# A three-block transformer kernel: expert stage and second attention merged into one block, with the first tile's steps, the gathers and the last key/value stores reordered

## The reference, cut to what matters

```
x = x + attention0(layernorm(x), ctx, ctx)   # 8 heads over the 512 axis, softmax over 64
x = x + experts(layernorm(x))                # gate x @ W_gate, top 2 of 8, mean of relu(x @ W_e + b_e)
x = x + attention1(layernorm(x), ctx, ctx)   # 32 query heads in 8 groups, head size 16, 64 keys
x = x + ffn(layernorm(x))                    # silu(x Wg + bg) * (x Wu + bu), inner size 1376, then Wd
```

## Time and profile before

| | us |
|---|---|
| median of 3 runs (lowest to highest) | 917.22 (916.62 to 917.77) |
| the profiled execution, its own time | 916.35 |
| its span, first to last instruction | 914.6 |
| PE busy | 861.1 (94%) |
| DVE, ACT, POOL busy | 442.5, 347.7, 296.6 |
| mean granted TensorE clock | 0.984 |
| first attention, first to last matmul (about) | 0 to 164 |
| experts, first matmul to last add | 173.5 to 303.2 |
| second attention, first matmul to the last scores | 307.0 to 525.7 |

### The profile page before, as it was taken

How to read it: one execution, slowest core, us unless ns; L and a number is a source line. 1 busy time by engine, 2 the same in 40 slices (tenths; PEclk the granted TensorE clock), 3 DMA queues, 4 the chain that set the end, 5 groups by cost and what they waited for, 6 DMA issues and landing times.

```text
span 914.6 us, 19686 instructions
## 1 busy us (share of the span) xinstructions
PE 861.1 (94%) x7537; PEld 698.9 (76%) x7537; DVE 442.5 (48%) x898; ACT 347.7 (38%) x567; POOL 296.6 (32%) x413
## 2 busy tenths in 40 slices
PE   6999998599999769999999899999999999999997
PEld 4788887478888757777777688887888788878885
DVE  3988886244444557887888741212221222222112
ACT  3555654233333245666666542221222122211111
POOL 3587885000000477777765231112020002002000
PEclk9999999799999898999999999999999999999999
DMA  8556666687553433554432341110030003002001
GB/s 284 175 185 235 214 206 228 217 271 247 165 173 127 150 93 126 150 154 130 137 91 56 100 160 40 47 43 1 13 104 24 0 12 104 1 1 92 1 1 46
DMA packets 55084, 105.24 MB, mean 115 GB/s; under 512 B 8050, under 2 KB 12146, under 8 KB 54866
## 3 DMA queue, kind: packets, MB, share of 16 engines
q1 hardware_dynamic: 48226, 84.98, 28.9%
q0 software_dynamic: 5120, 16.78, 5.5%
q10 hardware_dynamic: 1648, 2.23, 0.7%
HBM read 67.99 MB, written 35.98 MB: 114 GB/s over the span
## 4 chain that ended last, share of the span: by engine, by line
PE 61%; ACT 2%; DVE 1%; issue 1%; POOL 1%; DMA 1%; DVEq 0%; POOLq 0%
PE c_ps L1238 9%; PE c_ps L1240 9%; PE c_ps L1239 9%; PE c_bank L1719 4%; PE c_bank L1277 3%; PE c_bank L1276 3%; PE c_bank L1282 3%; PE c_bank L1720 3%; PE c_bank L1724 3%; PE c_bank L1779 3%; PE c_po L1795 2%; PE c_ps L1754 2%; PE c_po L1282 1%; PE c_po L1277 1%; PE c_po L1276 1%; ACT c_probT L1628 1%
## 5 line engine op out<-in xcount | busy, mean ns | idle before, releaser
L1315 DVE SCALAR_TENSOR_TENSOR d_hid<-c_ps,d_b_up,d_silu 128x512 f32<-128x512 f32 (+1 forms) x44 | 33.0, 750 | 229.7 <-PE c_ps L1240 229.7
L1238 PE MATMUL c_ps<-d_nT_hi,gate_up_hi 128*128 128x512 f32 (+1 forms) x352 | 140.1, 398 | 0.0
L1240 PE MATMUL c_ps<-d_nT_hi,gate_up_lo 128*128 128x512 f32 (+1 forms) x352 | 138.5, 394 | 0.0
L1239 PE MATMUL c_ps<-d_nT_lo,gate_up_hi 128*128 128x512 f32 (+1 forms) x352 | 138.3, 393 | 0.0
L1194 ACT ACTIVATE d_silu<-c_ps,d_b_gate 128x512 f32<-128x512 f32 (+1 forms) x44 | 30.3, 688 | 141.7 <-PE c_ps L1240 141.7
L1509 POOL DMA_INDIRECT c_y_in<-expert_results,y_at x32 | 36.6, 1145 | 145.2 <-POOLq L99 137.2
L1154 POOL TENSOR_TENSOR late_x<-late_x,d_b_down 128x512 f32<-128x512 f32 x16 | 21.6, 1380 | 188.0 <-DMA late_x<-x_after_attention 188.0
L1240 PEld LDWEIGHTS c_ps<-d_nT_hi,gate_up_lo 128*128 128x128 f32 (+1 forms) x352 | 65.2, 185 | 16.6
L1239 PEld LDWEIGHTS c_ps<-d_nT_lo,gate_up_hi 128*128 128x128 f32 (+1 forms) x352 | 65.4, 186 | 15.9
L1238 PEld LDWEIGHTS c_ps<-d_nT_hi,gate_up_hi 128*128 128x128 f32 (+1 forms) x352 | 65.2, 185 | 15.4
L1201 ACT ACTIVATE d_hid_hi<-d_hid 128x512 fp32r<-128x512 f32 (+1 forms) x44 | 27.8, 632 | 125.6 <-DVE d_hid L1315 125.6
(11 more groups left out here) (272 smaller groups left out, 1937.5 us busy)
## 6 DMA issues: line engine op xcount, KB each, us to landing
b_rows<-expert_rows SPq DMA_DIRECT2D x39, 256.0 KB, 2.8
expert_results<-b_result SPq DMA_DIRECT2D x39, 256.0 KB, 2.5
a_wstage<-L_ffn_W_e SPq DMA_DIRECT2D x16, 512.0 KB, 4.0
late_x<-x_after_attention SPq DMA_DIRECT2D x28, 256.0 KB, 3.9
c_stage<-gate_up SPq DMA_DIRECT2D x16, 344.0 KB, 3.2
out<-late_x SPq DMA_DIRECT2D x16, 256.0 KB, 2.9
x_after_attention<-late_x SPq DMA_DIRECT2D x12, 256.0 KB, 3.7
c_y_in<-x_after_attention SPq DMA_DIRECT2D x12, 256.0 KB, 2.8
```

Source lines behind the costliest of these rows:

```text
L1238: pe.matmul(bank[0:w, :], gu_hi[:, cols], nT_hi[:, g % 2, k, :], start=k == 0, stop=False)
L1239: pe.matmul(bank[0:w, :], gu_hi[:, cols], nT_lo[:, g % 2, k, :], start=False, stop=False)
L1240: mm = pe.matmul(bank[0:w, :], gu_lo[:, cols], nT_hi[:, g % 2, k, :], start=False, stop=k == KD - 1)
```

## The change

It does six things.

1. The experts no longer have a block of their own. `experts` returns functions for each engine, and the second attention's block runs them first. Their buffers lie on the same memory as the second attention's, their four PSUM banks are banks of the second attention, and their end is no barrier: PE waits for the DVE adds before it uses the last two banks, GpSimd and SP wait for the last stores (`ex.stored`), and GpSimd zeroes `kv` (before: DVE, L1930) once the last expert product is made. The clearing of the experts' semaphores between the stages is gone; a new set (`kept_`) adds one clearing at the program's end.
2. The first tile: its x comes by an earlier load; `add_first_rows` on DVE does the two adds of tile 0; GpSimd does `spread_keys(0)` and `scale_x2(0)` before `add_rows(1)` and `gather(2)`.
3. SP: the two halves of Wq are loaded during the experts into `late_x`; x tiles 2 to 5 and both halves of Wo follow behind the landing of `gather(0)`.
4. The splits of Wo move: ACT does both before the loop, DVE one before it and one in its first step. PE makes keys and values 0 to 6 before `transpose_x(0)` (before: 0 to 5), and those of tile 7 on the two sides of `make_q(0)`.
5. In each step PE does `transpose_probs(m, 0, 0)` before `scores(m, 1)`, and `gather(m + 5)` waits for `attend(m, 0, 1)`.
6. First attention: the stores of keys and values are no longer awaited in their block; `score` joins as a third staging buffer, cleared on DVE at m = TILES; `keep_kv(2)`, the first to use it, waits for that clearing.

The diff, cut to its core (the experts' own loops are the same but for indentation and for the names of semaphores and banks):

```diff
-        kv_stage = (qT, kT)
+        kv_stage = (qT, kT, score)
...
             def store_kv(i):
                 sp.wait_ge(kv_kept, i + 1)
-                sp.dma_start(shared["kv"][i, :, :], kv_stage[i % 2][:, 0:KV_COLS]).then_inc(kv_stored[i % 2], 16)
+                sp.dma_start(shared["kv"][i, :, :], kv_stage[i % 3][:, 0:KV_COLS]).then_inc(kv_stored[i % 3], 16)
...
             sp.wait_ge(front_zeroed, 16)
             for i in range(2):
                 sp.wait_ge(x1_stored[i], 8 * TILES)
-                sp.wait_ge(kv_stored[i], 8 * KV_LATE)
...
-                if i < 2:
-                    act.wait_ge(kv_cleared, 6)
-                want(act, kv_stored[i % 2], 16 * (i // 2))
-                act.activation(kv_stage[i % 2][:, 0:P], bank[:, 0:P], ACT.Copy).then_inc(kv_step, 1)
-                values = kv_stage[i % 2][:, P:KV_COLS].rearrange("p (b j r d) -> p b j r d", b=2, j=4, r=2)
+                if i < 3:
+                    act.wait_ge(kv_cleared, 3 * max(i, 1) + 3)
+                want(act, kv_stored[i % 3], 16 * (i // 3))
+                act.activation(kv_stage[i % 3][:, 0:P], bank[:, 0:P], ACT.Copy).then_inc(kv_step, 1)
...
                     dve.wait_ge(s_made, TILES)
+                elif i == 2:
+                    dve.wait_ge(pt_made, TILES)
                 dve.memset(blocks, 0.0).then_inc(kv_cleared, 1)
...
+                if m == TILES:
+                    clear_kv_stage(2)
...
+    sem, sb = c.sem, Placed(nc, "b_", shared["base"] + 2 * 4 * 2 * EXPERTS * DIM).sb
...
+    pt, py = banks[0:2], banks[2:4]
...
+            if 2 <= n < 4:
+                sp.dma_start(late.x[:, n - 2, :], shared["x1"][n - 2, :, :]).then_inc(late.x_loaded[n - 2], 16)
+            if 4 <= n < 6:
+                half = n - 4
+                sp.dma_start(late.x[:, 2 * half + 2:2 * half + 4, :], wq_v[:, 2 * half:2 * half + 2, :]).then_inc(proj_loaded[half], 16)
...
+            act.wait_ge(biased_made, b + 1)
+            want(act, stored[b % 3], 16 * (b // 3))
+            if b == 0:
+                for i in range(3):
+                    act.wait_ge(shared["kv_stored"][i], 16 * ((KV_LATE + 2 - i) // 3))
+            act.activation(result[:, b % 3, :], biased[:, b % 2, :], ACT.Relu, scale=0.5).then_inc(result_made, 1)
...
 
-            return score[:, n, :] if n < 2 else stage[:, :, :].rearrange("p s n -> p (s n)")[:, 0:1024]
+            if n == 2:
+                return stage[:, :, :].rearrange("p s n -> p (s n)")[:, 0:1024]
+            return (late.x[:, 2:4, :], late.x[:, 4:6, :], None, x_more[:, :, :])[n].rearrange("p s n -> p (s n)")
...
             def load_weights(n):
-                if n == 3:
-                    sp.wait_ge(proj_lo_made, 3)
-                src = (wq_v, wo_v)[n // 2][:, 2 * (n % 2):2 * (n % 2) + 2, :]
+                src = wo_v[:, 2 * (n % 2):2 * (n % 2) + 2, :]
...
             def load_x1(t):
+                if t in (X_RING, X_RING + 1):
+                    sp.wait_ge(proj_lo_made, 4)
...
 
-            for n in range(4):
-                load_weights(n)
+            def load_late_x(t):
+                sp.wait_ge(proj_lo_made, t // 2)
+                sp.dma_start(late.x[:, t, :], shared["x1"][t, :, :]).then_inc(late.x_loaded[t], 16)
+
+            ex.sync(sp)
+            sp.wait_ge(y_loaded[0], 32)
+            load_late_x(2)
+            load_late_x(3)
+            load_weights(2)
+            for i in range(3):
+                sp.wait_ge(ex.stored[i], 16 * ((BLOCKS + 2 - i) // 3))
+            load_weights(3)
+            load_late_x(4)
+            load_late_x(5)
             load_gate_up(0)
             load_gate_up(1)
             for t in range(X_RING, RING):
...
+            def clear_values():
+                pool.wait_ge(ex.y_made, BLOCKS)
+                pool.memset(kv[:, :, P:KV_COLS], 0.0).then_inc(values_zeroed, 1)
+                pool.wait_ge(values_zeroed, 1)
+                for r in range(2):
+                    pool.memset(kv[64 * r:64 * r + 64, :, P:KV_COLS].rearrange("p s (n r d) -> p s n r d", r=2, d=HD + 1)[:, :, :, r, HD:HD + 1], 1.0).then_inc(values_zeroed, 1)
+                pool.wait_ge(values_zeroed, 3)
...
             def add_rows(t):
+                if t == 1:
+                    pool.wait_ge(x2_ready, 1)
...
+            make_constants()
+            clear_values()
+            for i in range(3):
+                pool.wait_ge(ex.stored[i], 16 * ((BLOCKS + 2 - i) // 3))
             gather(0)
             gather(1)
-            make_constants()
-            add_rows(0)
-            gather(2)
+            spread_keys(0)
             scale_x2(0)
             add_rows(1)
+            gather(2)
+            scale_x2(1)
             gather(3)
-            scale_x2(1)
-            spread_keys(0)
             for m in range(TILES + 2):
                 if m == 0:
                     add_rows(2)
@@ -1576,6 +1601,7 @@
...
                 if m + 5 < TILES:
+                    pool.wait_ge(o_made, 4 * m + 2)
                     gather(m + 5)
...
+            ex.scalar(act)
             keep_kT(0)
+            high_weights(0)
             keep_kT(1)
-            high_weights(0)
-            keep_kT(2)
             high_weights(1)
-            for t in (3, 4, 5):
+            for t in range(2, 7):
                 keep_kT(t)
             norm_x(0)
             keep_high_x(0)
-            keep_kT(6)
+            high_weights(2)
             keep_q_rows(0)
             norm_x(1)
             keep_kT(7)
             keep_q(0)
+            high_weights(3)
             for m in range(TILES + 2):
                 if m + 1 < TILES:
...
                 if m < TILES:
                     exponent(m, 0)
-                if m == 0:
-                    high_weights(2)
                 if m + 1 < TILES:
                     keep_q_rows(m + 1)
                 if m < TILES:
@@ -1672,9 +1697,7 @@
                     exponent(m, 1)
                     if m == TILES - 1:
...
+                if t == 4:
+                    pe.wait_ge(ex.biased_made, BLOCKS - 1)
...
-                make_kv(t)
-            pe.wait_ge(const_made, N_CONST)
+            ex.tensor(pe)
+            for t in range(7):
+                make_keys(t)
+                make_values(t)
             transpose_x(0)
-            make_kv(6)
+            make_keys(7)
             make_q(0)
-            make_kv(7)
+            make_values(7)
             transpose_q(0)
             for m in range(TILES + 1):
                 if m < TILES:
...
                 if m < TILES:
+                    transpose_probs(m, 0, 0)
                     scores(m, 1)
-                    transpose_probs(m, 0, 0)
                     transpose_probs(m, 0, 1)
...
+            def add_first_rows():
+                dve.wait_ge(late.x_loaded[0], 16)
+                dve.wait_ge(y_loaded[0], 32)
+                dve.tensor_tensor(x[0], x[0], y_in[:, 0, :], ALU.add).then_inc(x2_added, 1)
+                dve.wait_ge(x2_added, 1)
+                dve.tensor_tensor(x[0], x[0], y_in[:, 1, :], ALU.add).then_inc(x2_ready, 1)
+
+            ex.vector(dve)
             keep_values(0)
+            low_weights(0)
             keep_values(1)
-            low_weights(0)
+            low_weights(1)
             keep_values(2)
-            low_weights(1)
             keep_values(3)
-            keep_values(4)
+            add_first_rows()
             sum_x2(0)
             average_x2(0)
+            keep_values(4)
             keep_values(5)
+            keep_values(6)
             keep_low_x(0)
+            low_weights(2)
             sum_x2(1)
             average_x2(1)
-            keep_values(6)
             keep_values(7)
             for m in range(TILES + 2):
                 if 0 <= m - 2 < TILES:
@@ -1955,7 +1990,7 @@
                 if m + 1 < TILES:
...
                 if m == 0:
-                    low_weights(2)
+                    low_weights(3)
                     sum_x2(2)
                     average_x2(2)
...
+    shared["base"] = SBUF_END - nc.sbuf_bytes_remaining
     with ExitStack() as stack:
+        kept = Ctx(nc, stack, "kept_")
+        shared["kv_stored"] = [kept.sem(f"kv_stored{i}") for i in range(3)]
+        stack.callback(kept.clear)
         with ExitStack() as moe:
             shared["ex23"] = [moe.enter_context(nc.sbuf_tensor(f"expert_{n}", [P, 2 * EXPERTS * DIM], F32R)) for n in ("hi23", "lo23")]
             first_attention(nc, shared, shared["layer0"], shared["layer1"])
-            late = LateBuffers(nc, stack, shared, shared["layer1"])
-            experts(nc, shared, shared["b_e"], late)
+        late = LateBuffers(nc, stack, shared, shared["layer1"])
         second_attention(nc, shared, shared["layer1"], late, a, out)
 
 

```

265 lines of the change are left out of this document (123 added, 142 removed).

## The result

In the first comparison the changed kernel takes 911.28 us (median of 4, 910.36 to 911.67) and the kernel before 917.5: a ratio of 0.992, 95% interval 0.9893 to 0.9946. The forecast was 905.2 with 901.5 to 908.8; the result lies outside. The profiled execution of the changed kernel took 911.67 us, span 909.7.

The account below looks back on a forecast made before the run. TensorE, busy 94% of the span, was taken as the bound, its time being work plus pauses. Terms 0.4 + 7.7 + 1.1 + 4.1 - 0.8 - 0.5 = 12.0 us saved gave 905.2 us, range 901.5 to 908.8.

Parts of the forecast that it names:

- First attention's end: End of the first attention's block: store wait gone, third buffer's clearing adds a pause; 0.4 us saved, bounds 2.4 saved to 0.5 lost.
- Experts to first scores: From the experts' end to the second attention's first scores: earlier gather landing, adds on DVE, earlier statistics; 7.7 us sooner.
- First step and steps 1 to 14: Second attention's loop: 1.1 us saved in the first step, 0.29 us in each of 14 later steps, 4.1 us.
- The gathers' new wait: GpSimd's loop gathers held until attend(m, 0, 1), some 1.2 us; claimed to cost nothing, at most 13 us over 11 steps.
- Last tile: Second attention's last tile: scores stand behind the exponent, so transpose_first waits longer; 0.8 us lost.
- The end: Program's end: one more semaphore clearing on SP; 0.5 us lost, bounds 0.2 and 0.8.
- The clock: TensorE's fall to 1.2 GHz in the loop's first step, counted as before; rival that it holds: 902.5 us, chance 0.27.
- The gain of the landing is not there: Rival: first gather lands after 6 us or Wo comes late, and loop steps gain half; 909.4 us, chance 0.15.

Follow-up runs that it names:

- e4: The changed kernel with, in the second attention's last tile alone, the second half's scores ahead of the first half's transposes again: 905.79 us.
- e1: The changed kernel run again unchanged, for a second trace: 905.56 us.
- e15: The changed kernel with third buffer cleared earlier, old order in the last tile, and DVE's first two Wq splits moved behind the first tile's statistics: 906.3 us.
- e16: As e15, with two copies of values put ahead of the two Wq splits and Wo's first half loaded earlier: 903.25 us.
- e7: The changed kernel with the second half's scores ahead of both first-half transposes in every tile of the second attention, as before the change: 908.99 us.
- e5: The kernel before the change run again unchanged, for a second trace: 939.61 us.

## Why the prediction was wrong

- **First attention's end**, forecast -0.4, measured +4.2; this carries 4.6 of the 7.1 us. Right was the pause: 1.9 us came with 1.8, the third copy waited for DVE. The failed step is the path behind it: "If only that wait went, the block would end when the table, the scatters and the last store's issue are through: 2.4 us saved", and "The block then ends at about 167.8". GpSimd's DRAIN of 2.68 us behind the last scatter was left out. With it the kernel before ended its block at 168.7 by GpSimd, not at 168.2 by SP's store wait. Removing that wait could save 0.15 us there, not 2.4, and nothing hid the pause. At full clock (e4) the way from the first late copy to the experts is 2.8 us longer, not 0.4 shorter. Of the +4.2, 0.5 lies ahead of everything that the change touches (the first late copy starts at 143.8, not 143.3), 2.8 is this, and the last 0.9 comes beside 10 us of low clock. A second error stood behind it: one trace of before was taken for the kernel's time. Its four other traces have 6.8 us of low clock there, take 3.1 us longer and are ended by the store wait; against them the term is about zero.
- **Experts to first scores**, -7.7 against -6.4. The failed step is when the gather goes out. Its second issue starts 6.0 us behind the last product where I had 5.0: the first issue goes out at 4.3 us and not at 3.65, since the store lands later, and the first issue takes 1.34 us, not 1.0, because a split of DVE runs beside it. The landing itself takes 4.3 us from the start of the second issue (forecast 3.9): both gathers in a row did no harm. I had weighed the Trainium skill's rule only against the adds: "SBUF — State Buffer", section "Who interferes with whom", where a VectorE instruction with two SBUF inputs contends with a GpSimd instruction that reads SBUF. There it cost DVE little (0.69 and 0.77 us here, 0.93 for the first in e1), and GpSimd's key copies took 1.73 in place of 0.76. e15 and e16 agree with the rule for GpSimd's scale. The 29.5 us of before is again one trace: its four others take 31.3 to 32.6, the changed kernel's four 22.9 to 23.6, so against them this stretch gains about 9 us.
- **First step and steps 1 to 14**, -5.2 against -5.5: right. A step went from 12.28 to 11.95; e7 shows the order as the cause. The forecast of 0.29 was 0.04 low. The first two steps together gave 1.1 us for the 1.4 forecast, so part of the match is two small errors that cancel.
- **The gathers' new wait**, costed at nothing: right on that, 11.95 us with it and without a gather alike. But I looked only for its price. What it brings, 21 us where the pauses are, is in no row of the first trace of before, and no case of mine had it. In the last comparison, where the kernel before is free of them by its time, the change gives 10.1 us for the 12.0 forecast.
- **Last tile**, +0.8 against +2.5. The 3.0 us pause came, the rest was mis-sized: the old order takes 14.1 to 14.6 us and the new one 15.5 to 17.1, about 1.9 by the means and 1.4 at a like clock. The 17.1 has 6.8 us of low clock, where I carried over the 3.4 of before.
- **The end**, +0.5 against +0.4: right.
- **The clock.** I counted one fall as certain or absent, in one place. The low stretches up to the last layer add up to 27 us in the first trace of before and to 34 in the changed kernel's, and the four runs of the first comparison have 0.979 to 0.981. I don't know why these four agree: later runs of the same kernel have 0.979 to 0.990. That e1's 905.56 lies close to the forecast of 905.2 is luck: the kernel before took 939 beside it.
- **The rivals.** "The gain of the landing is not there" (909.4) gave nearly the right time by the wrong cause: it did land in 4.3 us.

## What to carry to other kernels

Before you credit the removal of a wait at a block's end, list when every engine's own list is through, the sequencers' entries included: here another engine ended 0.15 us later, and the credit of 2.4 us was not there. Before a trace's idle or low-clock stretches become terms, look whether a second execution has them: here the same stretch of the unchanged kernel took 30.2 us in one trace and 33.2 to 33.5 in four. If TensorE pauses for "issue" inside many small products, look for a GpSimd gather issued at that moment and try to hold it behind them; here that was worth some 20 us where the pauses were, and cost nothing where they were not. When an operation moves past a loop's end, test the last iteration apart; the order that gains 0.33 us in each step lost 1.4 to 1.9 in the last tile.

## What the chip showed that was not expected

- A gather issued beside 64 products of 34 columns: two to three pauses of 0.45 to 0.49 us behind the 43rd to 45th product, a step of 13.9 us in place of 11.95 or 12.28, in some comparisons and not in others, on one and the same chip; a trace without pauses (the first of before) and one with them (e5) have the gather at the same place in the step.
- GpSimd's DRAIN at the end of a block took 2.68 us in each of 20 traces, and held the block's end in five of them.
- A two-input VectorE operation of 1.2 us beside GpSimd stretches a gather's issue from 0.95 to 1.86 us and a 128x1 operation from 0.23 to 1.10; a copy out of the accumulators does neither.
- TensorE's clock falls to the lower level in places that differ between executions of one program: the first fall behind 140 us is at 147.5, 155.0, 153.0 and 155.0 us in the changed kernel's four traces, the experts' first transpose at 177.7, 175.0, 173.3 and 176.7.
